# Attention with split fp32 products: values in two matmuls a tile, row sums on VectorE, low p on GpSimd, maxima by query tile, q and k spread by transfers

## The reference

```python
def _L1_attn_ref(x, gamma, w_qkv, w_out):     # 16 heads of 64
    xn = rms_norm(x, gamma)
    q, k, v = split(xn @ w_qkv)               # [b, 16, n, 64] each
    q = q * 64 ** -0.5
    sim = einsum('bhid,bhjd->bhij', q, k)
    attn = softmax(sim, axis=-1)
    out = einsum('bhij,bhjd->bhid', attn, v)
    return merge_heads(out) @ w_out
```

## Time and profile before

| | us |
|---|---|
| median of 3 runs | 2311.22 (2310.94 to 2311.55) |
| span of the profiled execution | 2302.3 |
| TensorE busy in the span | 2142.9 (93%) |
| VectorE busy | 1805.1 (78%) |
| ScalarE busy | 1587.2 (69%) |
| GpSimd busy | 1004.2 (44%) |

### The profile page before, as it was taken

One profiled execution on the slowest core, in us unless ns is written; L12 is line 12 of the kernel. 1 busy time (PEld: TensorE's weight loads), 2 busy tenths in 40 slices (PEclk: granted clock), 3 DMA queues, 4 the chain that ended last, 5 costly groups with the idle time before them and its releaser, 6 DMA issues.

```text
span 2302.3 us, 32776 instructions
## 1 busy us (share of the span) xinstructions
PE 2142.9 (93%) x9032; PEld 1504.7 (65%) x9032; DVE 1805.1 (78%) x2535; ACT 1587.2 (69%) x1898; POOL 1004.2 (44%) x636
## 2 busy tenths in 40 slices
PE   6999459998779999999999999999999999999997
PEld 4777237776647666666766666666666667666654
DVE  5888867886588888887888788788888878888555
ACT  4666426664427877777787777777777787777873
POOL 1000100003025566565565656556565655656672
PEclk7999769998679999999999999999999999999998
DMA  3210003110000000000000000000000000000000
GB/s 115 63 49 19 0 0 75 43 30 15 1 3 1 12 1 14 3 10 10 7 12 4 12 3 10 15 1 12 5 11 3 10 15 1 12 2 10 11 1 19
DMA packets 25125, 36.59 MB, mean 16 GB/s; under 512 B 11807, under 2 KB 14239, under 8 KB 23711
## 3 DMA queue, kind: packets, MB, share of 16 engines
q1 hardware_dynamic: 24958, 34.56, 5.8%
HBM read 32.99 MB, written 1.43 MB: 15 GB/s over the span
## 4 chain that ended last, share of the span: by engine, by line
PE 73%; DVE 13%; issue 7%; ACT 4%; POOL 2%; DVEq 0%; DMA 0%; ACTq 0%; POOLq 0%
PE ps L478 14%; PE ps L480 13%; PE ps L479 13%; PE ps L586 8%; PE ps L608 8%; PE ps L609 8%; DVE m_part L1219 2%; PE ps L460 2%; DVE p_l L1249 2%; POOL p_l L380 1%; ACT p_raw L926 1%; DVE m_part L1331 1%; DVE kb L1207 1%; PE ps L613 1%; PE ps L453 1%
## 5 line engine op out<-in xcount | busy, mean ns | idle before, releaser
L380 POOL TENSOR_TENSOR p_l<-p_raw,p_h 128x512 fp32r<-128x512 f32 (+1 forms) x512 | 836.9, 1635 | 651.3 <-ACT p_h L930 645.4
L1219 DVE TENSOR_REDUCE m_part<-ps 128x1 f32<-128x512 f32 x960 | 643.3, 685 | 191.0 <-PE ps L586 186.1
L926 ACT ACTIVATE p_raw<-ps 128x1024 f32<-128x1024 f32 x512 | 524.9, 1025 | 308.6 <-PE ps L609 283.6
L930 ACT ACTIVATE p_h<-p_raw 128x1024 fp32r<-128x1024 f32 x512 | 543.0, 1061 | 27.5
L1249 DVE TENSOR_TENSOR p_l<-p_raw,p_h 128x512 fp32r<-128x512 f32 x384 | 431.0, 1123 | 63.9 <-ACT p_h L930 49.8
L608 PE MATMUL ps<-qa,ka 128*128 128x512 f32 x1024 | 418.3, 408 | 7.4 <-DMA qb<-m_t 7.4
L478 PE MATMUL ps<-p_h,v_l 128*65 128x512 f32 x1024 | 404.4, 395 | 7.2 <-DVE p_l L1249 6.1
L609 PE MATMUL ps<-qb,kb 65*128 65x512 f32 x1024 | 407.5, 398 | 0.0
L479 PE MATMUL ps<-p_h,v_h 128*65 128x512 f32 x1024 | 402.6, 393 | 0.0
L480 PE MATMUL ps<-p_l,v_h 128*65 128x512 f32 x1024 | 402.4, 393 | 0.0
L586 PE MATMUL ps<-ka,qa 128*128 128x512 f32 x960 | 381.9, 405 | 8.0 <-DVE m_part L1219 5.6
(11 more groups left out here) (177 smaller groups left out, 2730.8 us busy)
## 6 DMA issues: line engine op xcount, KB each, us to landing
big<-g_scratch SPq DMA_DIRECT2D x64, 256.0 KB, 3.2
xnp<-r_scratch SPq DMA_DIRECT2D x15, 512.0 KB, 4.8
big<-in_w1T SPq DMA_DIRECT2D x1, 2048.0 KB, 9.0
big<-in_w2T SPq DMA_DIRECT2D x1, 2048.0 KB, 13.5
x<-in_xT SPq DMA_DIRECT2D x4, 256.0 KB, 3.6
qk_raw<-in_w_qkv SPq DMA_DIRECT2D x32, 32.0 KB, 1.9
out_xT<-x SPq DMA_DIRECT2D x4, 256.0 KB, 2.0
wv_raw<-in_w_qkv SPq DMA_DIRECT2D x8, 64.0 KB, 1.9
```

What stands on the lines that cost most here:

```text
L380: nc.gpsimd.tensor_tensor(p_l[:, g % 4, tiles, :], p_raw[:, g % 4, tiles, :], p_h[:, g % 4, tiles, :].bitcast(fp32), ALU.subtract).then_in ...
L926: af(p_raw[:, g % 4, :, :], ps[:, 2 * (g % 2):2 * (g % 2) + 2, :], ACT.Exp).then_inc(exp_done, 1)
L930: af(p_h[:, g % 4, :, :], p_raw[:, g % 4, :, :], ACT.Copy).then_inc(ph_done, 1)
L1219: nc.vector.tensor_reduce(m_part[:, ds(c, 1), it:it + 1].rearrange("p a t -> p (a t)"), ps[:, 4 + it % 2, :], AX.X, ALU.max).then_inc(s_ma ...
```

## The change

*Values.* `v_hl` holds v high and v low side by side in 128 columns. One matmul of it by p high gives v high by p high in the first 64 output rows and v low by p high in the other 64; a second one, v high by p low, adds to the first 64. `w_o` holds the 64 rows of a head twice, so that the output projection adds both halves; it is now done for every head.

*Row sums.* p has 17 slots of 512 queries, of which slot 8 is a partial sum. VectorE adds slots 0 to 7 in four pieces of 128 queries (`first_half_sum`, 1024 elements each) and then slots 8 to 16 (`whole_sum`, 1152 elements each), one piece a group. A matmul with ones adds over partitions. Sums are sent and inverted chunk by chunk.

*Low p* is computed by GpSimd for both tiles in every group. *p high* is a second exponential from PSUM, no longer a copy.

*Maxima* go by query tile: a pair of matmuls covers 1024 keys, one reduction takes both banks, and 32 pairs make a head. The maxima of the first four query tiles are closed and turned ahead of the other twelve.

*q and k.* ScalarE writes the high part of a quarter once, to a staging tile `qk_hi`, VectorE the low part to `qk_low`; six transfers (`move_qk`) copy them to qa (twice), ka (twice), kb and qb. There is one staging tile, and `wait_staging` lets a quarter be written when the six transfers of the one ahead have landed. The last two quarters are moved in the next window.

*v* is projected in three matmuls of 128 columns a tile instead of two of 256, and copied by ScalarE. The centred values and squares of later layer norms lie in p's tile.

The core of the diff:

```diff
-PROJECTED = {(3, 3): 0, (3, 4): 1, (3, 6): 2}
-MAXIMA_TILES = ((0, 2, 2, 3, 2, 2, 3, 2), (2,) * 8, (2,) * 8, (3, 3, 3, 2, 2, 2, 1, 0))
+PAIRS_OF_MAXIMA = ((0, 0, 1, 1, 1, 2, 1, 2), (1,) * 8, (1,) * 8, (1,) * 8)
+LOW_QK = {(3, 4): 0, (3, 6): 1}
+LATE_QK = {0: 2, 1: 3}
...
+            def move_qk(head, par, n, hi, lo):
+                sp.wait_ge(lo_done, chunk_of(head, n) + 1)
+                cols = chunk(n)
+                for dst, src in ((qa[par][0:DH, cols], hi[0:DH, :]), (qa[par][DH:128, cols], hi[0:DH, :]),
+                                 (ka[par][DH:128, cols], hi[DH:128, :]), (kb[par][0:DH, cols], hi[DH:128, :]),
+                                 (ka[par][0:DH, cols], lo[DH:128, :]), (qb[par][0:DH, cols], lo[0:DH, :])):
+                    sp.dma_start(dst.bitcast(fp32), src).then_inc(moved[par], 16)
...
-                tiles = slice(0 if g in POOL_GROUPS else 1, 2)
-                nc.gpsimd.tensor_tensor(p_l[:, g % 4, tiles, :], p_raw[:, g % 4, tiles, :], p_h[:, g % 4, tiles, :].bitcast(fp32),
+                nc.gpsimd.tensor_tensor(p_l[:, g % 4, :, :], slots(g), p_h[:, g % 4, :, :].bitcast(fp32),
...
+            def score_pair(head, par, q):
+                it, half = q // 2, q % 2
+                if q < 2:
+                    wait_moved(pe, head, par, 2 * q + 1)
+                pe.wait_ge(s_max, PRIME + MAXIMA * head + q)
...
-                    last = split_product(ps[0:DH + 1, sums_bank(c), :], v_h[:, par, jt, :], v_l[:, par, jt, :],
-                                         p_h[:, g % 4, j, :], p_l[:, g % 4, j, :], jt == 0, jt == NT - 1)
+                high(0, g == 0, False)
+                low(0)
+                low(1)
+                high(1, False, g == GROUPS - 1).then_inc(pv_done, 1)
...
-                af(p_h[:, g % 4, :, :], p_raw[:, g % 4, :, :], ACT.Copy).then_inc(ph_done, 1)
+                af(p_h[:, g % 4, :, :], s_t, ACT.Exp).then_inc(ph_done, 1)
...
+                if staged:
+                    wait_staging(act, head, par, n)
+                af(hi.bitcast(fp32r), ps[:, bank, :], ACT.Copy).then_inc(hi_done, 1)
...
+                nc.vector.tensor_reduce(p_raw[:, ACC, cols], p_raw[:, 0:FIRST_TILES, cols].rearrange("p a n -> p n a"),
+                                        AX.X, ALU.add).then_inc(half_sum, 1)
...
+                nc.vector.tensor_reduce(l_sum[:, cols], p_raw[:, ACC:NT + 1, cols].rearrange("p a n -> p n a"),
+                                        AX.X, ALU.add).then_inc(all_sum, 1)
...
+                nc.vector.tensor_reduce(m_part[:, it, half:half + 1], ps[:, 4:6, :].rearrange("p b n -> p (b n)"),
+                                        AX.X, ALU.max).then_inc(s_max, 1)
```

More of the change, by code:

```diff
@@ new lines, in scale, with window @@
+            def scale(head, c):
+                k = chunk_of(head, c)
+                pool.wait_ge(r_loaded, 16 * (k + 1))
+                pool.wait_ge(o_done, k + 1)
+                nc.gpsimd.tensor_tensor(o_raw[:, c % 2, :], o_raw[:, c % 2, :], r_bc, ALU.mult).then_inc(o_scaled, 1)
+            def window(pair, par, project):
+                head = 2 * pair + par
+                last = isinstance(head, int) and head == HEADS - 1
+                for c in range(NC):
+                    for g in range(GROUPS):
+                        low_part(head, c, g)
+                        if g == SCALE_GROUP:
+                            scaled = before(head, c, 2)
+                            if exists(scaled[0]) and not (last and c > 0):
+                                scale(*scaled)
+                        if (c, g) == V_SPLIT[par] and (par == 0 or project):
+                            low_v(head + 1, 1 - par)
@@ new lines, in score_pair, with turn_maxima @@
+            def score_pair(head, par, q):
[3 more added lines that the diff above has]
+                pe.wait_ge(s_max, PRIME + MAXIMA * head + q)
+                for b in range(2):
+                    last = mm(ps[:, 4 + b, :], qa[par][:, it * 128:it * 128 + 128], ka[par][:, chunk(2 * half + b)],
+                              start=True, stop=True)
+                last.then_inc(s_ps, 1)
+            def turn_maxima(head, par, part, bank):
+                tiles = slice(0, TPC) if part == 0 else slice(TPC, NT)
+                pe.wait_ge(m_ready, 2 * head + part + 1)
+                mm(ps[0:tiles.stop - tiles.start, bank, 0:128], m_col[par][:, tiles], ident[:, :],
+                   start=True, stop=True).then_inc(mt_ps, 1)
@@ new lines, in evicted @@
+            def evicted(head, pair, c, kind, n):
+                k = chunk_of(head, c)
+                if kind == "turn":
+                    pe.wait_ge(mt_done, 2 * (head + 1 - n) + n + 1)
+                elif kind == "sums":
+                    pe.wait_ge(l_done, k)
+                elif kind == "out":
+                    pe.wait_ge(out_add, k - 1)
+                elif kind == "v":
+                    pe.wait_ge(v_out, V_STEPS * (pair + 1) + n + 1)
+                elif kind == "qk":
+                    pe.wait_ge(hi_done, NC * (head + 2) + n + 1)
+                    pe.wait_ge(lo_done, NC * (head + 2) + n + 1)
@@ L774, in _ @@
+                end_out(NC, 5)
             layer_norm(0)
@@ new lines, in main_chunk @@
+                    exponentials(head, c, g)
+                    if g == COPY_GROUP and exists(summed[0]):
+                        copy_out(*summed)
+                    if c == 0 and g == 0 and late_project:
+                        high_qk(head + 1, 1 - par, NC - 1, spare_bank(NC - 1), qk_hi, True)
+                    for at, kind, n in plan:
+                        if at != g:
+                            continue
+                        if kind == "turn":
+                            turn_maxima(head + 1 - n, n, spare_bank(c))
+                        elif kind == "sums":
+                            row_sums(*summed, spare_bank(c))
+                        elif kind == "v":
+                            copy_v(pair + 1, n, spare_bank(c))
+                        elif kind == "qk":
+                            high_qk(head + 2, par, n, spare_bank(c), qk_hi, True)
@@ new lines, in invert, with add_out @@
+            def invert(head, c):
+                k = chunk_of(head, c)
+                dve.wait_ge(l_loaded, 16 * (k + 1))
+                if not (isinstance(k, int) and k == 0):
+                    dve.wait_ge(o_scaled, k)
+                nc.vector.reciprocal(r_col[:, c % 2, :], l_col[:, c % 2, :]).then_inc(r_ready, 1)
+            def add_out(head, c, bank):
+                dve.wait_ge(out_ps, chunk_of(head, c) + 1)
+                tt(x[:, chunk(c)], x[:, chunk(c)], ps[:, bank, :], ALU.add).then_inc(out_add, 1)
@@ new lines, in main_chunk @@
+                    if (c, g) == (NC - 1, GROUPS - 1) and not last:
+                        add_out(head, c - 2, spare_bank(c))
+                    if last:
+                        if (c, g) == (0, END_LATE_ADD):
+                            add_out(HEADS - 2, 2, 4)
+                        if g == END_INVERT:
+                            end_invert(c, spare_bank(c))
+                        if g == END_SCALE:
+                            end_scale(c)
+                    for _ in range(PAIRS_OF_MAXIMA[c][g] if has_next else 0):
+                        maximum(head + 1, next(pairs))
```

937 lines of the change are left out of this document (481 added, 456 removed).

## The result

The changed kernel takes 2569.86 us (median of 4 runs, 2565.83 to 2572.15) beside 2311.39 (2310.94 to 2311.76) for the kernel before: a ratio of 1.1123, interval 1.1107 to 1.1139. It is slower by 258 us, where 188 were forecast (2499; the range went to 2640). The profiled execution has a span of 2564.0 against 2302.3, and its own time of 2565.83 lies 1.8 above its span, not 9. In every run on record a time lies 2 to 3 us above its own span, and on other chips the kernel before took from 2303.4 to 2315.0 us. So the 8.9 us between the median and the span before are not what lies around the instructions: for the most part the profiled execution was a quicker one.

The account below looks back on a forecast made before the run. VectorE replaces TensorE as bound: 106.6 us a head plus 1.4 and 3.6 of waits, period 111.6; attention 1765 against 1577 (+188), span 2490, plus 9 gives 2499 us; range 2230 to 2640.

Parts of the forecast that it names:

- the price of a step: VectorE's sums over tiles: 1.66 ns an element instead of 1.04, from the 260 ns closing of maxima; 62.6 us a head.
- the small instructions: VectorE, each head: two closings, four reciprocals and low weights, 4.1 us.
- the overlap of queued ones: VectorE: queued instructions start 0.06 us before the one ahead ends; some 75 a head give back 4.6 us.
- double maxima: Twice a head two maxima pairs stand in one group; VectorE idles some 0.7 us for the second, 1.4 us a head.
- chain: Four moves of q and k before a maxima pair: 26.2 us against VectorE's 22.6 of work, adding 3.6 a head.
- The first window: The first head period of the attention loop, with no chain behind it: 108 us, against 111.6 in the other 14.
- the prologue: Before the attention loop: 4 us added for the moves of q and k.
- signals: Part of each move of q and k: signals and jitter, 0.3 to 0.8 us of 5.5.
- Rival B: Sums at the contiguous rate, TensorE the bound, chain remaining: period 97.5, 2279 us, range 2200 to 2330; chance 0.26.
- M: One move of q and k: six transfer issues on SP, landing and signals; 5.5 us, from 4.0 to 6.4.
- with the same 3.2 of waits 90.5: TensorE's 87.2 us of work a head plus the 3.2 of waits of the kernel before: 90.5 us.
- the 0.22 for faster: Chance given that the changed kernel is faster than before: sums at the contiguous rate, but for slow moves.

Follow-up runs that it names:

- adj: Changed kernel with p's two tiles of a group as neighbouring elements, half sums added by four more fp32 matmuls a head: 2397.77 us, ratio 1.0393.
- light_two_pool: Changed kernel with two staging buffers, sums over two tiles, and GpSimd making low p of one tile a group in heads 2 to 13: 2296.05 us.
- contig_two: Changed kernel with sums read from one contiguous run in heads 0 to 13 and two staging buffers: 2358.58 us, ratio 1.0204.
- adj_direct: Changed kernel with p in neighbouring pairs and q and k written in place, two transfers a quarter instead of six: 2330.98 us, ratio 1.0100.
- direct: Changed kernel with only q and k written in place, sums still at the step of a tile: 2535.83 us, ratio 1.0982.
- pairs: Kernel before with only the maxima of two tiles taken in one reduction over both score banks: 2330.66 us, ratio 1.0088.

## Why the prediction was right, and where its sizes were off

**The bound and the step: right.** TensorE waits for VectorE, VectorE has 106.2 us of own work in the head shown and 106.6 were forecast, and the price of a step came from one row of 260 ns. It was 1.68 against 1.66 ns an element. The sum itself was low in the kernel: 2.01 and 2.22 instead of 1.85 and 2.06, so 67.6 us of sums and not 62.6. The busy time of the head leaves 106.2 − 67.6 = 38.6 for all the rest, where 44.0 were put: the small instructions and the overlap of queued ones were off the other way. The small instructions took 1.6 instead of 4.1, and the overlap gave back about 6 instead of 4.6. That 106.2 came out beside 106.6 was luck: two errors cancelled.

**The waits: the term that was too small.** 5.0 us a head were forecast (1.4 of double maxima and 3.6 of chain), 9.9 are there. The period is 4.6 longer than forecast, and 14 × 4.6 = 64 are most of the 74 us by which the span was missed (2564.0 against 2490). The first window took 113.3 instead of 108, the stretch from the last closing to the end 152.5 instead of 146.3, and the prologue gave 2 back. The median was missed by 71 and not 74, as it lies 5.9 above the profiled span where 9 were put. In the chain itself 26.2 us became 29.2 (low part of quarter 0 done at 1118.6, last pair at 1147.8): four moves of 6.9, 5.7, 6.5 and 5.6 instead of 5.5, because SP issues a transfer of this kind every 0.64 us and not every 0.46 (3.1 us to the sixth in the second move, where 2.3 were put), and low parts can stand behind a sum (the third starts 0.45 us late). No row shows the 0.3 to 0.8 us that were put for signals: ScalarE starts 0.08 us after the landing (1132.45 and 1132.53). The clock was not in the working at all: after the two pauses shown, of 3.3 and 2.3 us, TensorE runs at 1.2 GHz for 6.1 and 3.5 us. How much of the 9.9 comes from that was not measured apart.

**Smaller terms.** Prologue: the first maxima close at 671.9 instead of 669.8, 2 us where 4 were put. GpSimd at 2.39 a group is under the 2.5 named as its threshold, and is no bound under the sums, as forecast.

**Rival B was mispriced, which the result hid.** For sums at the contiguous rate 2279 were given and a quarter of the chances. The nearest kernels are adj with 2398 (it has 3.4 us more of TensorE a head), and even without the chain 2331. The longer move explains little: at 56 us for each us of M, 6.2 instead of 5.5 is 38 us. The step of rival B that failed is "with the same 3.2 of waits 90.5". The 3.2 belonged to a kernel in which TensorE had 196 of 200 and nobody else over 165. With TensorE at 87, VectorE at 85 and GpSimd at 84.5 a head, TensorE's waits are 10 to 14 (96.9 in light_two_pool, 101.3 in contig_two, less 87.2); one pair of maxima in flight, the clock after pauses and GpSimd each have a part in them, and their shares stay open. So no complete version of this change that was tried is faster than the kernel before (light_two_pool, 0.5% faster, leaves out most of the sums and half of the low parts), and the 0.22 for faster rested on an engine's load taken for a period.

**What each part costs**, by medians, taken away in this order: the step 172 (changed to adj; 169 by the ratios; the four matmuls and the shorter second sum of adj are in it), staging by six transfers 67 (adj to adj_direct), what is left over the kernel before 22. In the other order staging is worth 34 (changed to direct) and the step 205 (direct to adj_direct). The 22 are of the size of what maxima by pairs cost alone (20, in the kernel before). That these are the same 20 us was not tested; in both kernels they stand mostly in the windows that project v (pairs has 99.7 and 103 to 104.5).

**Open.** The 0.1 us by which a strided sum in the kernel exceeds the isolated one beside GpSimd; the pause and the length of the windows that project v; and TensorE's 10 us of waits left in light_two_pool, where transfers (33 us of 1000 before score pairs) and waits that the profile names only as issue are mixed.
